# Expert stage of an attention and mixture-of-experts layer: half of each tile's transposes go from TensorE to a transposing DMA

## What is computed

```python
x = x + xattn(layernorm(x), ctx_1024, Wq1, Wk1, Wv1, Wk2, Wv2, Wo, bo)
mu, var = mean(x), mean((x - mu) ** 2)
h = (x - mu) / sqrt(var + 1e-5) * ln_gamma + ln_beta
shared_out = silu(h @ bit_quant(shared_w1).T) @ bit_quant(shared_w2).T
probs = softmax(h @ router_w.T);  e = argmax(probs);  p = max(probs)
routed_out = p * (silu(h @ bit_quant(expert_w1)[e].T) @ bit_quant(expert_w2)[e].T)
out = x + shared_out + routed_out
```

## Time and profile before

| | before |
|---|---|
| time, median of 3 runs | 820.25 us (819.57 to 821.07) |
| the profiled execution | 821.01 us |
| its span, first to last instruction | 819.3 us |
| mean granted TensorE clock, share of full | 0.96 |
| PE / DVE / ACT / POOL busy, share of the span | 83% / 78% / 74% / 70% |
| expert stage | about 697 us to the end |
| granted clock in the expert stage, 710 to 800 us | 1.00 |

### The profile page before, as it was taken

The page is one execution under the profiler, slowest core; times in us unless marked ns, Lnnn a source line. Parts: engine busy times, 40 slices in busy tenths (PEclk is TensorE's granted clock), DMA queues, the critical chain, the costliest instruction groups (busy, mean ns, idle before and its releaser), DMA issues.

```text
span 819.3 us, 22608 instructions
## 1 busy us (share of the span) xinstructions
PE 681.6 (83%) x7894; PEld 481.3 (59%) x7894; DVE 642.7 (78%) x1411; ACT 604.3 (74%) x1363; POOL 576.9 (70%) x684
## 2 busy tenths in 40 slices
PE   3688779898988999899988898989897765699993
PEld 2355546565656666666656565656565443577772
DVE  3879768888888889788888888888887546688883
ACT  3669567878787978788877878787876631688882
POOL 1356547787878788787878787878786866366664
PEclk9889889999999999999999999999998788899998
DMA  7289858898989999979899899998897842466541
GB/s 257 39 162 174 172 115 158 164 169 168 174 164 166 177 188 163 180 159 185 163 184 160 168 175 174 166 162 165 168 156 155 143 91 93 126 106 106 90 47 15
DMA packets 346307, 121.77 MB, mean 149 GB/s; under 512 B 309898, under 2 KB 341524, under 8 KB 346196
## 3 DMA queue, kind: packets, MB, share of 16 engines
q1 hardware_dynamic: 338388, 110.99, 71.1%
q0 software_dynamic: 7232, 8.79, 6.5%
q10 hardware_dynamic: 576, 0.54, 0.2%
HBM read 30.71 MB, written 14.71 MB: 55 GB/s over the span
## 4 chain that ended last, share of the span: by engine, by line
PE 41%; DVE 21%; issue 13%; DMA 10%; ACT 7%; POOL 7%; SPq 1%; ACTq 1%; DVEq 0%; POOLq 0%
PE FB L358 10%; DMA pt<-p_split 9%; PE TBK L1460 5%; PE S L1388 4%; DVE neg_max L1205 4%; PE S L1563 4%; POOL p_split L571 3%; DVE FB L943 2%; DVE above L948 2%; PE S L1564 2%; ACT k_st L736 2%; ACT p_split L773 2%; DVE v_st L973 2%; DVE hn L1055 2%; POOL g_lo L622 2%
## 5 line engine op out<-in xcount | busy, mean ns | idle before, releaser
L571 POOL TENSOR_TENSOR p_split<-probs,p_split 128x512 f16<-128x512 f32 x256 | 300.2, 1181 | 64.3 <-ACT p_split L773 62.0
L811 ACT ACTIVATE probs<-S,neg_max 128x512 f32<-128x512 f32 x256 | 174.9, 683 | 16.2 <-DVE neg_max L1205 15.0
L773 ACT ACTIVATE p_split<-probs 128x512 f16<-128x512 f32 x256 | 161.0, 629 | 19.2 <-DMA pt<-p_split 17.8
L1205 DVE TENSOR_REDUCE neg_max<-S 128x1 f32<-128x512 f32 x256 | 171.1, 679 | 0.6 <-PE S L1388 0.2
L358 PE MATMUL FB<-xt_hi,w_split 128*128 128x256 f16 x768 | 142.3, 277 | 3.2 <-DVE xt_lo L970 2.9
L1404 PE MATMUL O<-v_st,pt 128*128 128x64 f16 x1024 | 114.6, 195 | 27.2 <-DMA pt<-p_split 26.9
L1404 PEld LDWEIGHTS O<-v_st,pt 128*128 128x128 f16 x1024 | 93.2, 99 | 61.3 <-DMA pt<-p_split 36.7
L1405 PE MATMUL O<-v_st,pt 128*128 128x64 f16 x1024 | 113.9, 195 | 0.0
L1406 PE MATMUL O<-v_st,pt 128*128 128x64 f16 x1024 | 113.9, 194 | 0.0
L1388 PE MATMUL S<-k_st,q_st 64*128 64x512 f16 x768 | 107.1, 385 | 1.1 <-ACT probs L811 1.1
L358 PE MATMUL FB<-xt_lo,w_split 128*128 128x256 f16 x384 | 106.2, 276 | 0.0
(11 more groups left out here) (227 smaller groups left out, 1815.2 us busy)
## 6 DMA issues: line engine op xcount, KB each, us to landing
w_raw<-in_L_ffn_expert_w SPq DMA_DIRECT2D x16, 512.0 KB, 4.5
w_split<-rows SPq DMA_DIRECT2D x39, 132.0 KB, 2.2
c_in<-in_ctx SPq DMA_DIRECT2D x16, 256.0 KB
x_in<-in_x SPq DMA_DIRECT2D x16, 256.0 KB
xb<-in_x SPq DMA_DIRECT2D x16, 256.0 KB, 3.5
pt<-p_split SPq DMA_TRANSPOSE x256, 3.3
out<-rest SPq DMA_DIRECT2D x15, 256.0 KB, 2.5
k_st<-in_L_xattn_Wk SPq DMA_DIRECT2D x2, 512.0 KB, 7.5
```

Of the source, the lines that this page charges most:

```text
L571: g.tensor_tensor(p_split[n % HL_RING][:, 1, :], probs[n % PROBS_RING][:, :], p_split[n % HL_RING][:, 0, :], ALU.subtract).then_inc(p_lo_r ...
L773: a_(p_split[g % HL_RING][:, 0, :], probs[g % PROBS_RING][:, :], ACT.Copy).then_inc(p_hi_ready, 1)
L811: a_(probs[n % PROBS_RING][:, :], S[n % 4][:, :], ACT.Exp, bias=neg_max[:, n % 4:n % 4 + 1], accum_out=sums[:, n % UNITS:n % UNITS + 1]).t ...
L1205: v.tensor_reduce(neg_max[:, n % 4:n % 4 + 1], S[n % 4][:, :], AX.X, ALU.max, negate=True)\
```

## The change

For each tile TensorE turns only the rounded half (two transposes in place of four), ScalarE copies 256 columns in place of 512, and SyncE issues a transposing DMA from `g_rows` straight to the second half of `e_ht`, with a semaphore of its own for each of the four buffers, for which `up` waits. The loads of the rows run three tiles ahead of these DMAs in the same queue. Nothing else is different.

```diff
+LEAD = 3
+        e_ht_in = [sem(f"e_ht_in{i}") for i in range(HT_RING)]
-        e_columns = FB[0][:, 0:D].bitcast(F16)
+        e_columns = FB[0][:, 0:P].bitcast(F16)
 # SyncE
+            def turn_rests(a):
+                sp.wait_ge(row_in[a % RING], 16 * (a // RING + 1))
+                if a >= HT_RING:
+                    sp.wait_ge(e_up_full, a - HT_RING + 1)
+                sp.dma_start(e_ht[a % HT_RING][:, DC:2 * DC, :], g_rows[a % RING][:, 0:D].bitcast(F16)[:, D:2 * D], transpose=True)\
+                    .then_inc(e_ht_in[a % HT_RING], 16)
+            for a in range(LEAD):
+                load_rows(a)
             for a in range(SLOTS):
-                if a >= RING:
-                    sp.wait_ge(e_out, a - RING + 1)
-                load_rows(a)
+                if a + LEAD < SLOTS:
+                    if a + LEAD >= RING:
+                        sp.wait_ge(e_out, a + LEAD - RING + 1)
+                    load_rows(a + LEAD)
+                turn_rests(a)
 # ScalarE, copy_columns
-                a_(e_ht[a % HT_RING], e_columns.rearrange("p (b t) -> p b t", t=P), ACT.Copy).then_inc(e_ht_ready, 1)
+                a_(e_ht[a % HT_RING][:, 0:DC, :], e_columns.rearrange("p (b t) -> p b t", t=P), ACT.Copy).then_inc(e_ht_ready, 1)
 # TensorE, turn
-                for c in range(2 * DC):
+                for c in range(DC):
 # TensorE, up
                 pe.wait_ge(e_ht_ready, a + 1)
+                pe.wait_ge(e_ht_in[a % HT_RING], 16 * (a // HT_RING + 1))
                 if a >= 2:
                     pe.wait_ge(e_u_low, a - 1)
                     pe.wait_ge(e_u_high, a - 1)
```

## The result

| | before | changed |
|---|---|---|
| time, median | 819.91 us (818.61 to 821.07, 4 runs) | 829.08 us (827.71 to 830.25, 4 runs) |
| the profiled execution's span | 819.3 us | 827.5 us |
| pace of the tiles 5 to 37 | 2.566 us | 2.795 us |

The ratio is 1.0103, 95% interval 1.0073 to 1.0133: the change makes the kernel slower by 1.0%, about 8.5 us. The prediction had the direction and one of two causes; it put the size at +3.3 us.

The account below looks back on a forecast made before the run. TensorE's sequencer was taken as the bound: 38 tiles x (0.10 for the wait - 0.01 for fewer transposes) = +3.4 us, start -0.1, together +3.3 on 820.25, so 823.6 us; range 818.8 to 829 us.

Parts of the forecast that it names:

- the third rival: SyncE becomes the bound, from an issue of 1.46 us on: 825 us at 1.5, 835 at 1.78; chance 0.12.
- the forecast's own sum: 38 tiles x (0.10 - 0.01) = +3.4 us, start -0.1: +3.3 us, 823.6 us; ends 821.9 to 825.6.
- What bounds the kernel: Expert stage: a chain within TensorE's sequencer sets when `up` starts; the array idles 0.41 us in the tile read.
- The removed transposes: TensorE, two of four a tile: 0.11 us less array work, off the path; gain 0.01 us a tile, at most 0.04.
- The added wait: In `up` for `e_ht_in`: a second EVENT_SEMAPHORE a tile, costing 0.10 us, with 0.09 and 0.12 as ends.
- SyncE keeps up, with 0.2 us to spare: SyncE's load-and-transpose round takes 2.44 us against TensorE's 2.67; 0.2 us charged for a late fourth tile, ends 0 and 1.0.
- The signs foretold: Changed trace: two EVENT_SEMAPHORE ahead of each `up`, pace 2.64 to 2.68 us, no TensorE wait for DMA behind four tiles.

Follow-up runs that it names:

- e1: The kernel before with one more wait in `up`, for `row_in` of the same tile, long met; 1.0048 of the time before, pace 2.676 us.
- e2: The kernel before with two transposes a tile and a 256-column copy, rests not turned, no DMA or wait added; 0.9997 of before, pace 2.604 us.
- e6: The kernel before with TensorE's waits spread so each rides on an instruction, a repeated one dropped, no DMA changed; 0.9892 of before, pace 2.299 us.
- e11: e6 with two transposes a tile and a 256-column copy, rests not turned, no DMA; 0.9861 of before, pace 2.201 us.
- e4: The changed kernel without the wait for `e_ht_ready` in `up` that `turn` has already made, save at two tiles; 1.0077 of before, pace 2.700 us.
- e9: e4 with the row loads at fixed addresses, so SyncE reads no register for them; 1.0010 of before, pace 2.580 us.
- e3: The kernel before with the changed kernel's SyncE loads and transposing DMAs, written to a buffer nobody reads or waits for; 1.0015 of before, pace 2.73 us.
- e10: e6 with the changed kernel's two transposes and SyncE DMAs, row loads at fixed addresses; 0.9855 of before, pace 2.208 us.

## Why the prediction was right and where it was wrong

**The number.** The direction was right. The size was not: +3.3 us was forecast, with +1.6 to +5.3 as its ends, and +8.5 was measured. The measured 829.08 us lies outside these ends (821.9 to 825.6 us), at the very end of the stated range of 818.8 to 829; 1.0103 times the 820.25 us of before is 828.7. The range reached that far only because it took in the near half of the third rival, which had a chance of 0.06. That the time fell there is luck, as far as the forecast's own sum goes.

**What bounds the kernel.** Right: a chain within TensorE's sequencer, beside which the array works. e1 and e2 are the two halves of the proof, and e6 is its strongest part: 8.9 us come out of waits that nobody was late for.

**The removed transposes.** Right: taken at 0.01 us a tile, measured as nothing in e2. The same edit gives 0.098 us a tile in e11, which agrees with the 0.11 that was worked out for the array.

**The added wait.** Right in mechanism and size: 0.10 taken, 0.11 measured in e1, and the second EVENT_SEMAPHORE as foretold from the earlier trace rows. The figure of the Trainium skill ("Runtime: NRT & Kernel Launch", section "Instruction fetch mechanics", some 20 cycles for an instruction) gave an estimate of 67 ns for four instructions fewer, most of what the wait costs. It does not show here: e2 gains nothing.

**SyncE.** Here the prediction failed, in the term "SyncE keeps up, with 0.2 us to spare", charged with 0.2 us. Three numbers in it were too small. The issue was taken at its median, 1.23 us; its mean in the changed kernel is 1.38, because of the long ones. The row L463 showed a maximum of 4.4 us, and for a queue that must sustain a pace the mean counts; over the 256 issues of that line it is 1.39. The register load of SyncE was taken from the undisturbed burst at the start, and reaches 0.76 us behind transposing issues. And 2.5 us to landing was the figure of L472 alone, the shortest of three lines; L463 had 3.3 at the median in the kernel before, and L457 4.1. In the changed kernel it is 3.3. The round came to 2.71 us on average and to 2.9 over several tiles in a row, where 2.44 was reckoned and TensorE needs 2.67: there was nothing to spare. With no lead, each long round of SyncE becomes a wait of TensorE that later short rounds do not give back. This term measures 5.5 us (e4 to e9, 2.7 to 8.2 by the intervals) where 0.2 was charged, with 1.0 as its upper end. The third rival had the mechanism, with a threshold of 1.46 us for each issue: that was too strict, since it took the register load as constant and the issue as even.

**The sum.** The steps between the measured kernels are 0.8 us from before to e9 (within its interval nothing), 5.5 us from e9 to e4 for SyncE's round, and 2.1 to 2.8 us from e4 to the changed kernel for the wait. They add up to the measured difference because each starts where the one before ends, so their sum proves nothing. Whether the two causes add is open: one wait costs 3.9 us alone (e1) and 2.1 to 2.8 us in the changed kernel, which would fit SyncE covering a part of it, but each of these numbers has about 2 to 3 us to either side.

**The signs foretold.** Two EVENT_SEMAPHORE, L1550's successor two at a time, transposing issues of 1.2 us at the median: seen. The array idle for about 0.6 us ahead of `up`: 0.51 in the quiet tile. A pace of 2.64 to 2.68 and no wait for a DMA behind the first four tiles: not seen, 2.795 and waits at the tiles 6, 7, 8, 12 and 16.

**Open.** Why one transposing issue in five holds SyncE for 1.8 to 2.4 us was not settled; e3 excludes only the wait for `up`. That SyncE's register load grows with them was seen, and not tried apart.

## What to carry to other kernels

Before taking work off an engine, look whether its array or its sequencer sets the pace: a short idle stretch put down to "issue" at the same place of each round, with register loads and stand-alone waits in front of it, meant the sequencer here, and then one wait more cost and two matmuls fewer gave nothing. Place waits so that each rides on an instruction that comes anyway; drop those that an earlier wait of the same engine covers. A queue that must keep pace is to be reckoned with the mean of its rounds, long issues included, and needs a lead or a clear margin over the engine that it feeds.

## What the runs showed of the hardware that I had not expected

- A wait already met is not free on TensorE: 0.11 us as an EVENT_SEMAPHORE (e1). With each wait on an instruction that comes anyway, three EVENT_SEMAPHORE fewer gave 0.27 us a tile until the array was the bound (e6 against before). What such a wait still costs, e6 cannot show, since there the array sets the pace.
- The queue in front of the array took at least 32 instructions without stopping the sequencer.
- The issue of a transposing DMA holds SyncE for 1.2 us at the median for 256 columns, as for 512 (L472) or 1024 (L463); L457, also 1024 columns, takes 1.78. One in five of the changed kernel's takes about 2 us; of L472's 30 none takes over 1.4.
- The transposing transfers themselves slowed nothing that could be measured: with a DMA share of 0.91 in e10 and 0.74 in e11 (740 to 760 us) the paces differ by 0.007 us a tile.
